# Attention opening with row-band tables: other batches prepared behind the scores, first rows in 32 transfers after all stores

## The reference

```
# ffn0: top-1 of 8 experts, D=128, F=512
y = gelu(t @ w1[e] + b1[e]) @ w2[e] + b2[e]      # e = argmax(softmax(t @ switch_w + switch_b))
# attn0: 16 heads of 8, relative positions in 64 buckets
q, k, v = heads(x @ Wq + bq), heads(x @ Wk + bk), heads(x @ Wv + bv)
pos_k = heads(rel_embeddings @ Wk + bk)
scores = (q @ k.T + take(q @ pos_k.T, bucket(i - j)) + take(k @ pos_k.T, bucket(i - j)).T) / sqrt(24)
out = layernorm(softmax(scores) @ v @ Wo + bo + x) * ln_scale + ln_bias
```

## Time and profile before

| | |
|---|---|
| median of 3 runs | 749.17 us (748.17 to 756.85) |
| the profiled execution | 749.62 us |
| its span, first to last instruction | 747.9 us |
| mean granted clock of TensorE | 0.901 |
| busy: PE, PE weight loads | 577.3, 416.1 us |
| busy: DVE, ACT, POOL | 532.4, 453.4, 210.1 us |
| DMA | 127.81 MB, mean 171 GB/s |

### The profile page before, as it was taken

One profiled execution on the slowest core, in us unless ns is written; L12 is line 12 of the kernel. 1 busy time (PEld: TensorE's weight loads), 2 busy tenths in 40 slices (PEclk: granted clock), 3 DMA queues, 4 the chain that ended last, 5 costly groups with the idle time before them and its releaser, 6 DMA issues. The chain is left out here.

```text
span 747.9 us, 17250 instructions
## 1 busy us (share of the span) xinstructions
PE 577.3 (77%) x5361; PEld 416.1 (56%) x5361; DVE 532.4 (71%) x1881; ACT 453.4 (61%) x983; POOL 210.1 (28%) x271
## 2 busy tenths in 40 slices
PE   4399992079999999999999997551996673678770
PEld 3298881046666666767676765441995342346450
DVE  7543421957787777999899995873224799867897
ACT  3245661047888888999899996450552534376723
POOL 5756432301912720470400000034343200211200
PEclk9999997588999999999999999655898797799995
DMA  9988667799899989999845420834554000000001
GB/s 237 254 264 248 193 206 204 212 313 342 224 339 354 301 299 313 246 214 358 225 135 142 135 66 9 249 85 130 167 187 118 7 1 0 0 1 1 1 1 57
DMA packets 125900, 127.81 MB, mean 171 GB/s; under 512 B 27963, under 2 KB 102883, under 8 KB 124915
## 3 DMA queue, kind: packets, MB, share of 16 engines
q1 hardware_dynamic: 116946, 97.19, 46.1%
q0 software_dynamic: 4704, 27.88, 9.9%
q10 hardware_dynamic: 4160, 1.63, 1.1%
HBM read 68.37 MB, written 48.79 MB: 157 GB/s over the span
## 5 line engine op out<-in xcount | busy, mean ns | idle before, releaser
L1725 DVE CUSTOM_DVE_ANT_0 l0am_prob<-l0am_ps_s,l0am_bias 128x512 f32<-128x512 f32 x256 | 166.7, 689 | 33.0 <-PE l0am_ps_s L1799 23.8
L1642 ACT ACTIVATE l0am_prob<-l0am_prob,l0am_neg_top 128x512 f32<-128x512 f32 x256 | 171.4, 723 | 6.0 <-DVE l0am_neg_top L1725 6.0
L1812 PE MATMUL l0am_ps_t<-c_ident,l0am_prob 128*128 128x128 f32 x1024 | 129.8, 277 | 0.4 <-DVE l0am_probT L1712 0.4
L1812 PEld LDWEIGHTS l0am_ps_t<-c_ident,l0am_prob 128*128 128x128 f32 x1024 | 112.0, 142 | 16.3 <-issue 8.0
L646 ACT ACTIVATE l0f_h<-l0f_psU,l0f_experts 128x128 f32<-128x128 f32 x212 | 60.5, 368 | 76.7 <-PE l0f_psU L973 76.5
L1712 DVE COPY l0am_probT<-l0am_ps_t 128x512 f32<-128x512 f32 x128 | 82.2, 683 | 1.4 <-PE l0am_ps_t L1812 1.4
L839 DVE COPY l0f_xsT<-l0f_psT 128x128 f32<-128x128 f32 x53 | 15.4, 291 | 91.4 <-PE l0f_psT L963 86.1
L1799 PE MATMUL l0am_ps_s<-l0am_ks,l0am_qs 32*128 32x512 f32 x512 | 75.7, 647 | 3.8 <-DVE l0am_neg_top L1725 2.6
L1636 ACT COPY l0am_probT<-l0am_ps_t 128x512 f32<-128x512 f32 x128 | 68.6, 589 | 10.6 <-PE l0am_ps_t L1812 10.6
L541 POOL DMA_INDIRECT token_results<-l0f_ys,l0f_token_i x53 | 51.0, 962 | 74.0 <-DVE l0f_ys L849 69.2
L1826 PE MATMUL l0am_ps_cg<-l0am_probT,l0am_v 128*9 128x128 f32 x2048 | 67.9, 273 | 1.8 <-DVE l0a_heads L1736 1.8
(11 more groups left out here) (342 smaller groups left out, 955.5 us busy)
## 6 DMA issues: line engine op xcount, KB each, us to landing
l0am_bias<-near_terms SPq DMA_DIRECT2D x128, 192.0 KB, 4.7
near_terms<-l0am_near POOLq DMA_DIRECT2D x6, 3072.0 KB, 13.2
l0f_mine<-l0f_experts SPq DMA_DIRECT2D x53, 256.0 KB, 2.4
near_terms<-l0am_near SPq DMA_DIRECT2D x4, 1536.0 KB, 7.9
l0o_rows_k<-position_k SPq DMA_DIRECT2D x12, 512.0 KB, 6.9
l0f_experts<-in_L_ffn_w SPq DMA_DIRECT2D x2, 2048.0 KB, 21.0
position_q<-l0o_rows SPq DMA_DIRECT2D x16, 256.0 KB, 4.7
position_k<-l0o_rows SPq DMA_DIRECT2D x16, 256.0 KB, 5.9
```

The costliest lines, as they stand in the source:

```text
L1642: nc.scalar.activation(prob[:, k, :], prob[:, k, :], ACT.Exp, bias=neg_top[:, k:k + 1], scale=-1.0)\
L1725: dve.tensor_tensor_reduce(out=prob[:, k, :], in0=ps_s[:, j, :], in1=bias[:, j, at:at + S], scale=-1.0, scalar=HUGE, op0=ALU.add, op1=ALU.min,
L1812: last = pe.transpose(ps_t[:, BANK_OF[j], i, :], prob[:, u % SLOTS_, i * P:(i + 1) * P], ident[:, :])
```

## The change

The opening is rewritten. Instead of extended weights, q and k are projected with Wq and Wk themselves (two products of 512 columns for a batch), and the tables come from products of 32 contracted rows: `spread` holds the position rows for four heads, so one product gives all 32 table rows of one quarter of the heads. Eight such products make a batch (`BATCH_ROWS`), issued in pairs in different row bands, one bank for ACT and one for DVE. Nothing else of what is computed changes.

- Constants: `QUARTERS` = 4, `BATCH_ROWS` = 8; the margins between row chunks in the table go.
- FFN phase: `turn_weights`, `extend` (slots 11 and 13), `extend_positions`, `copy_extended` go; `multiply_bias` is two products in slot 12. Project q in slot 21, k in 22; product pairs in slots 23 to 26; plain q and k rows are stored in the steps of slots 24 and 25, tables in those of 26 to 29, two in each. The 32 row loads of batch 0 follow behind the last slot, after a wait for all eight stores. POOL no longer waits for its last scatters; SP does in the next phase. The blocks end without POOL's drain.
- Score phase before the quads: DVE sets a constant in `v`, builds near, updates and normalises batch 1 only (its deviation by Ln and Exp on ACT instead of Sqrt and a reciprocal); PE multiplies values of batch 0. The bias tile is cleared by ACT, not POOL. SP: far stores first, gathers, tiles, closing weights, then as before, but the second group's near store leaves right behind the first bias loads.
- POOL scales and adds the results of batches 2 and 3 and normalises them; DVE takes their statistics in quads 1 to 3.
- In the quads, by the tables below: turn, project, row pairs and values of batches 1 to 3, 18 quads besides quad 0; quad 0 turns and projects batch 1 and has its first row pair.
- PE: `turn_heads` stands behind the transposes; the second and the third transpose group wait for ACT's and DVE's late copy. DVE: one copy of two banks for the last two heads, then `close_heads(q-4)`, two additions, the late copy, two additions.
- Near terms of batches 1 to 3: POOL builds 32 of the 64 query rows with half the corners and all bands, stores, builds the other 32, stores, and waits for both.

```diff
+LATE_STEPS = {0: [("turn", 1), ("project", 1), ("rows", BATCH_ROWS)], 5: [("values", 1)],
+              7: [("turn", 2)], 8: [("project", 2)], 13: [("values", 2)],
+              17: [("turn", 3)], 18: [("project", 3)], 23: [("values", 3)]}
+LATE_STEPS |= {first + n: [("rows", BATCH_ROWS * b + 2 * n)] for b, first in ((1, 0), (2, 9), (3, 19)) for n in range(QUARTERS) if first + n}
+STATS_QUAD, REFINE_QUAD = 1, 4
+STACK_STEPS = {0: [(1, 0), (1, 1)], 9: [(2, 0)], 10: [(2, 1)], 25: [(3, 0)], 26: [(3, 1)]}
+FAR_STEPS = {5: (1, 0), 7: (1, 1), 16: (2, 0), 18: (2, 1), 32: (3, 0), 34: (3, 1)}
+ROW_STEPS = {2: [(1, 0, 0), (1, 1, 0)], 3: [(1, 2, 0), (1, 3, 0)], 4: [(1, 0, 1), (1, 1, 1)], 5: [(1, 2, 1), (1, 3, 1)]}
+ROW_STEPS |= {first + pair: [(b, pair, 0), (b, pair, 1)] for b, first in ((2, 14), (3, 27)) for pair in range(TABLE_CHUNKS)}
...
                 if opening:
-                    for cn in range(len(STORE_SLOTS), BATCH_CHUNKS):
-                        opening.store_chunk(sp, cn)
-                        opening.load_rows(sp, cn - 2)
+                    sp.wait_ge(aside.blocks_out, 16 * aside.BLOCK_STORES)
+                    for side in range(2):
+                        opening.wait_stored(sp, 0, side)
+                    for pair in range(TABLE_CHUNKS):
+                        for side in range(2):
+                            opening.load_rows(sp, 0, pair, side)
...
+    def multiply(self, pe, cn, banks):
+
+        b, i = divmod(cn, BATCH_ROWS)
+        side, first = divmod(i, QUARTERS)
+        pe.wait_ge((self.q_ready, self.k_ready)[side], b + 1)
+        for n, bank in enumerate(banks):
+            r = slice(32 * (first + n), 32 * (first + n) + 32)
+            pe.matmul(bank, self.aside.spread[r, side, :], self.qk[r, side, :], start=True, stop=True,
+                      tile_position=(32 * (first + n), 0)).then_inc(self.tab_psum, 1)
...
                 for b in range(1, B):
                     if b == 1:
                         for g in range(GROUPS):
-                            pool.wait_ge(first_near_out[g], 16)
-                    near_build(pool, b, between).then_inc(near_pool, 1)
-                    pool.wait_ge(near_pool, b)
+                            near_stored(pool, 0, g)
                     for k, (q0, q1) in enumerate(LATER_PIECES):
+                        rows_arrived(pool, b, 0)
+                        near_corners(pool, q0, q1).then_inc(near_steps, 1)
+                        pool.wait_ge(near_steps, len(LATER_PIECES) * (b - 1) + k + 1)
+                        for pair in range(TABLE_CHUNKS):
+                            rows_arrived(pool, b, pair)
+                            last = near_bands(pool, RUNS_OF[pair], q0, q1)
+                        last.then_inc(near_pool, 1)
+                        pool.wait_ge(near_pool, len(LATER_PIECES) * (b - 1) + k + 1)
                         store_near(b, q0, q1)
-                        pool.wait_ge(near_out, 16 * (len(LATER_PIECES) * (b - 1) + k + 1))
+                    pool.wait_ge(near_out, 16 * len(LATER_PIECES) * b)
...
+                    for t in range(T4 if n else 0):
+                        q = T4 * (n - 1) + t
+
+                        sp.wait_ge(neg_ready, 4 * q + 4)
+                        if t == 0:
+                            near_stored(sp, b, g)
+                        load_bias(n, t)
                         if n == 1 and t < 2:
                             store_first_near(2 + t)
...
+                        for later, pair, side in ROW_STEPS.get(q, ()):
+                            if pair == 0:
+                                sp.wait_ge(*((near_pool, len(LATER_PIECES) * (later - 1)) if later > 1 else (near_dve, 1)))
+                                opening.wait_stored(sp, later, side)
+                            opening.load_rows(sp, later, pair, side)
...
                 for q in range(QUADS + 4):
                     if 2 <= q < QUADS + 2:
-                        copy_turned(4 * (q - 2) + 2)
-                        copy_turned(4 * (q - 2) + 3)
+                        copy_last_two(q - 2)
+                    if 4 <= q:
+                        close_heads(q - 4)
                     if q < QUADS:
+                        if q == 0:
+                            late_copies(q, ("project",))
                         add_terms(4 * q)
                         add_terms(4 * q + 1)
-                    if 3 <= q < QUADS + 3:
-                        close_heads(q - 3)
-                    if q < QUADS:
+                        late_copies(q, ("project", "rows", "values") if q else ("rows",))
                         add_terms(4 * q + 2)
                         add_terms(4 * q + 3)
+                        later_statistics(q)
...
                     if j == 3:
                         pe.wait_ge(copied_act, 2 * q + 1)
                     elif q:
-                        pe.wait_ge(*((copied_dve, 2 * q), (copied_act, 2 * q), (copied_dve, 2 * q - 1))[j])
-                    if j == 2 and q + 1 in late:
-                        pe.wait_ge(rows_ready, late[q + 1] + 1)
+                        pe.wait_ge(*((copied_dve, q), (copied_act, 2 * q), (copied_dve, q))[j])
+                    if j in (1, 2):
+                        wait_late_copies(pe, q + 1, j == 1)
```

More of the change, by code:

```diff
@@ L453, in store_blank @@
             queue.dma_start(xs_dram[bass.ds(end, P), :], c["blank"][:, e, 0:XS_COLS]).then_inc(stored, 16)
-        with nc.Block() as block:
+        with nc.Block(no_gpsimd_drain=opening is not None) as block:
             @block.sync
@@ L1652, in _ @@
                 for q in range(QUADS + 3):
-                    if q in late:
-                        copy_rows(late[q], ps_row)
+                    late_copies(q, ("turn", "project", "rows") if q else ("turn", "project"))
                     if 1 <= q <= QUADS:
```

726 lines of the change are left out of this document (355 added, 371 removed).

## The result

| | before | after |
|---|---|---|
| median of eight runs each | 748.82 us (745.41 to 756.85) | 756.02 us (750.88 to 758.85) |
| ratio after/before | | 1.0083 [1.0050, 1.0117] |
| the profiled execution, its span | 749.6, 747.9 us | 757.8, 756.0 us |
| first score added | 163.80 | 158.54 |
| quad 16 added | 245.77 | 246.42 |

A forecast was written before the change was run, and what follows sets the result against it. It took PE's stream to bound the quads, with SP's queue holding the block's start and near terms holding quad 16. Quad 16 1.2 us later plus 1.9 behind it gave 752.7 profiled, 752.3 beside the median, range 737 to 764.

The forecast's parts named there:

- Block start: End of FFN: 32 row loads issued in one run on SP, block starts at 131.0, 1.3 later; bounds 128.5 and 135.
- FFN: FFN up to the update: PE loses some 4.7 us of work, but POOL's gather limits the gain to 0.9.
- Hand-over: Block start to first score: first addition at 156.2, not 163.80, so 7.6 us gained.
- Quads: Attention's quads: PE's stream sets 4.13 us plain, 5.65 with row products, 5.36 values, 4.66 turn, 6.2 project.
- the stall: In row quads: PE's second transpose group waits 0.55 us for ACT's copy of the row products.
- (d): Rival in row quads: row pairs don't overlap, 0.96 us more each, total 756; counted within the forecast's 0.45.
- Near terms of batch 1: Before quad 16: POOL starts at 195, last store lands at 240.3, quad 16 waits 6 us, bounds 0 and 14.
- Rival (a): At quad 16: near terms come in time, quad 16 starts at 241.0, total 744.3; chance 0.2.
- (b): Rival in quads 2 and 4: SP's queue backs up, quad 16 11 us later, some 762, if POOL starts after 202; chance 0.18.
- Tail: From quad 16 on: 210.2 us against 208.3 before, so +1.9.
- (c): Rival: FFN's gain passes through, late quads don't stall, no wait at quad 16; about 735 to 739; chance 0.17.
- verdict of no change: Whole kernel: the time stays within the 2% step, 15 us, that tells a change; chance 0.77.

The follow-up runs named there:

- e9_before_two: Kernel before, with ACT issuing the last 12 of the 32 first row loads on its own queue; 749.1 us, ratio 0.9988.
- e1_stores: Changed kernel, with SP storing batch 0's eight table copies three slots earlier; 754.7 us, ratio 1.0047.
- e6_nochain: Changed kernel without the near stores of batches 1 to 3, their bias read from batch 0's terms; 744.5 us, ratio 0.9928.
- e4_fewbands: Changed kernel, with POOL building only 8 of 32 bands of batch 1's near terms in each half; 756.6 us, ratio 1.0065.
- e11_before_nodrain: Kernel of e9_before_two, with POOL's program also ending without its wait for the last scatters and without the drain; 748.5 us, ratio 0.9932.
- e2_eight: Changed kernel, with first rows loaded in 8 transfers and near terms stored from 32 neighbouring partitions per head group; 756.5 us, ratio 1.0051.

## Why the prediction came out right, point by point

- **Block start** (forecast +1.3, measured +5.0; the mean of the changed kernels with all 32 loads on SP is 133.4, of three old ones 130.0, so +3.4). The 20.6 us for 32 issues became 22.3, mostly since the first four took 3.9. "The block can't end before SP has issued its queue" was half of it: POOL's end stood at about the same time (`e9_before_two`). And the step from the last copies to the first load left out that the eighth copy needs the first buffer again, whose store SP issues only then: six buffers for eight copies. That wait was 0.8 to 5.0 us in seven profiles, and taking it away moved the first load by 0.5 in the pair. The upper bound of 135 held it, by 0.3 us.
- **FFN** (0.9 gained up to the update; measured 3.2 in the pair, 2.9 between the means of nine new and five old profiles, 77.15 and 80.04). The gather did move with the loop, by 1.8 (72.23 against 74.01), and landed sooner. Without this gain the block start would, by the same order of steps, have been later still.
- **Hand-over** (first score at 156.2, −7.6; measured 158.5, −5.3, and −7.2 between the means, 157.3 and 164.5). From block start to first score 25.2 forecast, 23.9 measured. The order of events was as said: near build, projections at the lower clock, DVE's copy of the keys at 157.87, 0.7 before the first addition.
- **Quads.** Plain 4.13, measured 4.15; values 5.36, 5.31; turn 4.66, 4.64; project 6.2, 6.08; quads 0 and 1 12.7, 12.9. Row quad 5.65, measured 5.38: the mis-sized term is the stall, 0.28 and not 0.55. The products cost 0.95 for the pair, as charged, which settles (d). What the prediction took from the Trainium skill (TensorEngine Tiling (Array Packing), Performance Considerations, PSUM Bottleneck), that emptying PSUM may become the limit of tiled products, shows here as these 0.28 us for each row quad, no more.
- **Near terms of batch 1** (wait 6, bounds 0 and 14; measured 3.9). POOL started at 200.6 and not 195, its half builds took 11.3 us for 32 bands where I put 16.9 and 15.1 with corners and waits (14.7 and 13.0 with their corners), so the second store left at 229.7 and had landed when the bias load left at 242.17, forecast 240.3. Late start and short build offset each other. Rival (a) was 3.9 us from true; the start, 1.4 before the point from which (b) was to decide, shows that this was close.
- **Tail** from quad 16 to behind quad 63 (210.2 against 208.3, so +1.9; measured 214.2 against 211.6, +2.6, the last quad taken as plain). The difference is nearly right, both sums are too low: 1.1 too much for four row quads, and nothing for what quads 24 to 62 lose beyond 4.15 each, 3.9 us, most of it in 35 to 40, when batch 3's stores are under way; the old kernel loses 3.6 in quads 21 to 24 and 40. These late losses differ from one execution to the next (1.6 in `e1_stores`). That the row loads, stores and bias transfers of every batch meet in one resource was nowhere in the sum; (b) had it for one place. `e6_nochain` shows what the near stores cost, and `e4_fewbands` that the wait moves when they come closer together.
- **Behind the scores** nothing was forecast, and the pair shows +4.9: 0.7 of it comes with the change in every profile, some 2 came from an old profile shorter than its kind, and the rest stays open.
- **(c)** falls: quad 16 waits and the row quads stall. But one of its signs came, the update before 77 (76.09, with a mean of 77.15), since the FFN's gain was partly real.

So the verdict of no change came out right, and attention's +3.1 against +3.2 measured is in part luck: a missed wait, a missed lock and a missed shared resource are in it, and gains of about the same size. Of the 3.7 us between forecast and measured median none lies in attention by this pair; what lies behind the scores covers it. It would have been better to read the DMA share beside PE's, in the view of the earlier trace rows on to 340 us, before taking PE's stream for the only limit.

## What to carry to other kernels

When a block's end is late, list the last event of every engine's program before you price one of them: with two locks at about the same time, opening one alone shows nothing, as `e9_before_two` does, and the gain comes only with the second, as in `e11_before_nodrain`. Work moved from a bare stretch behind a busy one is paid for in what the busy stretch is short of, here mostly buffers and transfers, and PE only for the row products themselves. And a serial run of issues is shortened most cheaply by a second queue that is idle then, not by larger transfers in another layout, unless the layout is good for those who read it next.

## What the runs showed of the hardware that I had not expected

- A store of 1.5 MB took 5.4 us out of every fourth partition (148.20 to 153.62) and 9.0 out of 32 neighbouring ones (135.50 to 144.54), both on SP's queue with little else under way: some 290 and 174 GB/s. Under load, on POOL's queue, it took 10 to 12, as long as twice the bytes out of all 128. The Trainium skill (SBUF — State Buffer, Door 1: The DMA port swizzle) offers a reason: partitions 0 to 31 reach 8 of the 16 ports, and every fourth of 128 reaches all by its formula; it gives 189 GB/s for partitions 0 to 31 at 1 MiB. The measured 174 GB/s is near that figure, and the strided store is faster, as the rule has it, though by 1.7 and not 2. No run here shows the ports themselves. The rule would have told ahead that both my experiments with neighbouring partitions give up a good part of a store's rate.
- With two near stores of 3 MB issued within 7 us, one issue on SP's queue took 8.27 us instead of 0.6, at a DMA share of 0.99 (`e4_fewbands`), and everything behind it in SP's program came that much later. That the full engines hold up the issuing one is the likely reason; the profile doesn't name it.
- With POOL's wait for its scatters and its drain, the block of the old kernel started 11.2 to 12.6 us behind the start of the last scatter in four profiles; without them it started 7.0 behind it in `e11_before_nodrain` and 5.8 in `e2_eight`, where other queues may still have been the last.
